# Score products and maxima of a windowed attention, contracted over 64 partitions in place of 128

## The reference

```python
scores = jnp.einsum('bhnqd,bhnkd->bhnqk', qw, kw) * scale + pos_bias[None, :, None]
probs = jax.nn.softmax(scores, axis=-1)
ow = jnp.einsum('bhnqk,bhnkd->bhnqd', probs, vw)
...
merged = merged / jnp.clip(counts, 1.0, None)[None, None, :, None]
ctx = merged.transpose(0, 2, 1, 3).reshape(Bb, Ss, Hid)
return ctx @ Wo + bo
```

## Time and profile before

| | |
|---|---|
| Time, median of 3 runs | 781.19 us (776.79 to 782.27) |
| The profiled execution | 777.4 us, its span 775.7 us |
| TensorE matmuls busy | 680.1 us, 88% |
| VectorE / ScalarE / GpSimd busy | 499.4 / 371.6 / 433.3 us |
| TensorE's mean granted clock | 0.948 of 2.4 GHz |

### The profile page before, as it was taken

How to read it: one execution, slowest core, us unless ns; L and a number is a source line. 1 busy time by engine, 2 the same in 40 slices (tenths; PEclk the granted TensorE clock), 3 DMA queues, 4 the chain that set the end, 5 groups by cost and what they waited for, 6 DMA issues and landing times. The chain is left out here.

```text
span 775.7 us, 34452 instructions
## 1 busy us (share of the span) xinstructions
PE 680.1 (88%) x13946; PEld 544.1 (70%) x13946; DVE 499.4 (64%) x1624; ACT 371.6 (48%) x546; POOL 433.3 (56%) x482
## 2 busy tenths in 40 slices
PE   4699999999999999999999999988999999999000
PEld 1467777767776777677777677768999999999000
DVE  6735656666675665756657557665788766766076
ACT  2133443443434434434343342445677777776058
POOL 6820334545545545455464454456777777777645
PEclk8889999999999999999999999998999999999555
DMA  6884436435454353443643534013434534332196
GB/s 156 241 266 122 126 92 170 130 88 151 123 146 138 94 169 112 120 143 112 164 135 86 159 110 131 26 38 88 147 101 117 157 101 112 103 106 69 48 381 269
DMA packets 84029, 103.61 MB, mean 134 GB/s; under 512 B 15937, under 2 KB 70593, under 8 KB 83873
## 3 DMA queue, kind: packets, MB, share of 16 engines
q1 hardware_dynamic: 73792, 82.26, 36.6%
q0 software_dynamic: 8640, 17.84, 7.2%
q10 hardware_dynamic: 1440, 1.31, 0.5%
HBM read 60.12 MB, written 40.79 MB: 130 GB/s over the span
## 5 line engine op out<-in xcount | busy, mean ns | idle before, releaser
L786 DVE TENSOR_REDUCE neg_max<-score_ps 128x16 f32<-128x1024 f32 x109 | 133.3, 1223 | 132.8 <-PE score_ps L1200 128.9
L295 POOL DMA_INDIRECT slots<-rows_sb,slot_at x128 | 128.0, 1000 | 154.6 <-PE o_ps L1253 119.2
L680 ACT ACTIVATE prob<-scoret_ps 128x1024 f32<-128x1024 f32 x112 | 114.6, 1023 | 143.6 <-PE scoret_ps L1200 143.6
L545 POOL DMA_INDIRECT results<-scaled_sb,result_at x142 | 136.2, 959 | 43.1 <-issue 35.2
L1253 PE MATMUL o_ps<-v_sb,prob 128*32 128x18 f32 x7168 | 90.6, 187 | 9.4 <-issue 8.6
L1253 PEld LDWEIGHTS o_ps<-v_sb,prob 128*32 128x32 f32 x7168 | 76.6, 110 | 22.0 <-issue 14.4
L713 ACT CAST w_slot<-wgu_sb 128x1024 fp32r x71 | 74.6, 1051 | 0.3 <-issue 0.3
L1237 PE MATMUL scoret_ps<-max_rows,half 128*64 128x512 bf16 x448 | 68.2, 382 | 5.3 <-DMA max_rows<-maxt_sb 5.1
L1220 PE MATMUL scoret_ps<-bias_hl,fold 128*64 128x512 f16 x448 | 70.2, 393 | 0.9 <-ACT prob L680 0.9
L1200 PE MATMUL scoret_ps<-blocks,stack 128*64 128x256 f16 x920 | 70.3, 274 | 0.1
L659 ACT COPY v_sb<-bank 64x512 f32<-64x512 f32 (+1 forms) x64 | 36.0, 563 | 68.4 <-PE bank L1190 38.6
(11 more groups left out here) (179 smaller groups left out, 1482.2 us busy)
## 6 DMA issues: line engine op xcount, KB each, us to landing
stack<-scratch SPq DMA_DIRECT2D x32, 512.0 KB
blocks<-scratch SPq DMA_DIRECT2D x126, 128.0 KB
scratch<-qk_hl SPq DMA_DIRECT2D x120, 128.0 KB
xin<-slots SPq DMA_DIRECT2D x71, 130.0 KB
blocks<-results SPq DMA_DIRECT2D x16, 512.0 KB, 6.3
x_sb<-in_x SPq DMA_DIRECT2D x16, 256.0 KB
out<-y_sb SPq DMA_DIRECT2D x16, 256.0 KB, 3.9
results<-scaled_sb,result_at POOLq DMA_INDIRECT x142, 2.6
```

Source lines behind the costliest of these rows:

```text
L295: nc.gpsimd.indirect_dma_start(slots, bass.IndirectOffsetOnAxis(ap=slot_at[:, k % 2, n:n + 1], axis=0), rows_sb[:, k % 2, n // TT, n % TT, ...
L545: pool.indirect_dma_start(results, bass.IndirectOffsetOnAxis(ap=result_at[s % RBUF][:, t:t + 1], axis=0), scaled_sb[:, s % RBUF, t, :], No ...
L680: act.activation(prob[:, (par + u) % 2, :], scoret_ps[:, :, :].rearrange("p b c -> p (b c)"), ACT.Exp).then_inc(exp_done, 1)
L786: dve.tensor_reduce(neg_max[:, par, v, :], ps[:, :, :].rearrange("p b (h k) -> p (b h) k", k=W), AX_X, ALU.max, negate=True).then_inc(max_ ...
```

## The change

The contraction is cut in two halves of 64 partitions. Each group of heads g gives two matmuls for each window where it gave one: n = 0 takes heads j = 0 and 1 on partitions 0 to 63 and writes bank 0, n = 1 takes j = 2 and 3 on partitions 64 to 127 and writes bank 1. Each has 128 columns. With the two windows (column halves of the array) that makes four tiles of 64 x 64. The maxima are laid out so that those of bank 0 come on partitions 0 and 1 and those of bank 1 on 64 and 65, and their matmul contracts over 64 partitions too. The order of heads, the mask, `neg_max` and the DMAs follow.

```diff
 def place(j, g):
-    return 4 * g + j
+    return 8 * (j // 2) + 2 * g + j % 2
...
-        neg_max = sb("neg_max", [P, 2, NU, H])
+        neg_max = sb("neg_max", [P, 2, 2, NU, H // 2])
...
-        max_rows = sb("max_rows", [P, NU * H, 64], BF16)
+        max_rows = sb("max_rows", [P, NU * H // 2, 64], BF16)
...
-                        sp.dma_start(max_rows[a:a + 1, :, :], maxt_sb[:, 64 * a:64 * a + 64]).then_inc(rows_in, 16)
+                        sp.dma_start(max_rows[a:a + 65:64, :, :], maxt_sb[:, 64 * a:64 * a + 64]).then_inc(rows_in, 16)
...
-                link(pool.memset(half[:, :], 1.0))
-                link(pool.affine_select(out=half[:, :], in_=half[:, :], compare_op=ALU.is_ge, fill=0.0, base=0,
-                                        pattern=[[1, P]], channel_multiplier=-64))
-                pool.affine_select(out=half[:, :], in_=half[:, :], compare_op=ALU.is_ge, fill=0.0, base=63,
-                                   pattern=[[-1, P]], channel_multiplier=64).then_inc(first_constants, 1)
+                windows = half[:, :].rearrange("p (a q) -> p a q", a=2)
+                link(pool.memset(half[:, :], 0.0))
+                link(pool.affine_select(out=windows, in_=windows, compare_op=ALU.not_equal, fill=1.0, base=0,
+                                        pattern=[[-1, 2], [0, 64]], channel_multiplier=1))
+                pool.affine_select(out=windows, in_=windows, compare_op=ALU.not_equal, fill=1.0, base=-64,
+                                   pattern=[[-1, 2], [0, 64]], channel_multiplier=1).then_inc(first_constants, 1)
...
-                    dve.tensor_reduce(neg_max[:, par, v, :], ps[:, :, :].rearrange("p b (h k) -> p (b h) k", k=W),
+                    dve.tensor_reduce(neg_max[:, par, :, v, :], ps[:, :, :].rearrange("p b (h k) -> p b h k", k=W),
...
                     for g in range(G):
-                        for a in range(2):
-                            t0 = UNITS[u][a]
-                            last = pe.matmul(ps[64 * a:64 * a + 64, g // 2, (g % 2) * 4 * W:(g % 2 + 1) * 4 * W],
-                                             stack[:, par, a_of, g, t0:t0 + W],
-                                             blocks[:, par, b_of, g, :, t0:t0 + W],
-                                             start=False, stop=True, skip_group_check=True)
+                        for n in range(2):
+                            k = slice(64 * n, 64 * n + 64)
+                            for a in range(2):
+                                t0 = UNITS[u][a]
+                                last = pe.matmul(ps[64 * a:64 * a + 64, n, 2 * g * W:2 * (g + 1) * W],
+                                                 stack[k, par, a_of, g, t0:t0 + W],
+                                                 blocks[k, par, b_of, g, 2 * n:2 * n + 2, t0:t0 + W],
+                                                 start=False, stop=True, skip_group_check=True)
...
-                            pe.matmul(scoret_ps[rows, n, :], half[:, rows],
-                                      max_rows[:, u * H + 8 * n:u * H + 8 * n + 8, :].rearrange("a h q -> a (h q)"),
+                            pe.matmul(scoret_ps[rows, n, :], half[64 * n:64 * n + 64, rows],
+                                      max_rows[64 * n:64 * n + 64, 8 * u:8 * u + 8, :].rearrange("p h q -> p (h q)"),
...
-                    pe.transpose(bank[0][0:NU * H, 0:P], neg_max[:, par, :, :].rearrange("p u h -> p (u h)"),
+                    pe.transpose(bank[0][0:NU * H, 0:P], neg_max[:, par, :, :, :].rearrange("p n u h -> p (n u h)"),
```

## The result

The changed kernel takes 790.33 us, the median of 5 runs (788.97 to 799.95), against 779.92 before (776.79 to 782.27). The ratio is 1.015, 95% interval 1.011 to 1.019: slower by one and a half per cent where 764 us and a gain were forecast, and just outside the range, which ended at 790.

A forecast was written before the change was run, and what follows sets the result against it. TensorE's instruction list was taken to bound each attention step. Turned side gains 33.3 us, straight side loses 14.4, code costs 2: 17 off 781 gives 764 us, range 724 to 790.

The forecast's parts named there:

- the one on code: Whole kernel: 3,584 more TensorE instructions make some 14 more code packets, costing 1.1 to 3.9 us, taken as 2.
- The check in the part on products: Product groups: values put out records 10 ns each, 16 products need 14.5 ns each, so instruction supply is no bound.
- The row halves run side by side: Maxima: four matmuls on two row and two column halves run in one round, 0.217 us against 0.433.
- The change of the row count: Between TensorE groups: switching between 128-row and 64-row tiles costs 0.10 us, bounded by 0 and 0.164.
- exposed loads: First weight load after a shape change: 0.02 us into long matmuls, 0.05 into short ones, 12.3 us in all.
- the turned side: Turned maxima and products: gains 2.92 us a step less 0.84 for shape changes, 33.3 us in 16 steps.
- the straight side: Straight products: gain 1.41 us a step, shape changes cost 0.72 and 1.65; 14.4 us lost in 15 steps.
- The cheap: Rival: a row-count change costs 0.05 us or nothing, giving 746 or 715 us; chance of 715 to 750: 0.18.
- the dear change: Rival: a row-count change costs up to 0.164 us, giving 788 us; chance of 775 to 790: 0.14.
- the halves in turn: Rival: row halves load weights in turn, 815 us, or matmuls take turns too, 839; chance of 800 to 839: 0.12.
- The covers: Reduction's split output, the maxima's DMA onto two partitions and its prologue clearing stay hidden and cost nothing.
- anything else: Remaining outcomes, such as TensorE's clock falling with sparser work; chance 0.04.

The follow-up runs named there:

- e5: The kernel before, unchanged, profiled again on another job's chip: 782.23 us (one run).
- e6: The changed kernel, unchanged, run again on another job's chip: 795.30 us, 1.013 of the kernel before.
- e11: The kernel before with the change on the turned side alone and the values in matmuls of 64 queries, not 32: 764.71 us, 0.978 of before.
- e4: The changed kernel with the values in matmuls of 64 queries in place of 32, half as many instructions there: 0.980 of the kernel before.
- e3: The kernel before with the change on the turned side alone (maxima and turned products over 64 rows), straight products as before: 1.011 of before.
- e1: The kernel before with products in 16 matmuls of 128 columns, still over all 128 rows (3,584 extra instructions, no new tile shape): 1.017 of before.
- e10: The changed kernel with straight bias ahead of turned maxima and values in matmuls of 64 queries: 752.13 us, 0.960 of the kernel before.

## Why the prediction was wrong

**The step that failed** is the one on code: "14 packets cost 1.1 to 3.9; I take 2." The change cost about 29 us of idle time (1.82 us a step in 16 steps, e5 and e6; 1.77 of it at the boundaries of packets), the lower clock behind some of the stops included; the first pair of profiles has 2.31 us a step. The count of 14 was right. The price was taken as a mean per packet from the kernel before, as if each packet brought its own small share of idle time. But it goes by a threshold: nearly nothing where 256 instructions last over about 3.9 us, and about the difference where they don't. So it isn't the 14 packets more that cost, but that every packet has less time: 45 of 84 stretches fall under the threshold where 17 of 73 did. The rows taken from before could have shown it. Its plain turn stood at 4.08, just above, but its stops at the boundary already came to 0.88 us a step, 14 us in 16 steps, four of them over 1 us, while the prediction counted 1.1 to 3.9 for packets of the same size; and 200 against 232 instructions in a shorter turn is a sum that could be done beforehand. The check in the part on products, 10 ns an instruction in the values, was of how fast TensorE takes instructions that are there, not of how fast they come.

**What held.** The row halves run side by side, which no row of before had shown. The change of the row count costs 0.10 as taken (a guess from the nearest row, so partly luck), with exposed loads of the sizes taken; 28.8 was left of a step where 28.7 was forecast (29.82 - 1.12). By the same prices the turned side without the straight one should leave a step 0.24 shorter (2.92 - 0.84 - 0.72 = 1.36 gained, against 1.12); measured it is 0.11 (e11 to e4) and nothing (e3 to e6). So the straight side earns about nothing on the array and costs half of the added code; that it isn't a loss comes from the products, which are cheaper than forecast (a group of four rounds takes 0.22, not 0.23, and its exposed load 0.02 to 0.03, not 0.05). The cheap and the dear change, and the halves in turn, were each refuted by the first timeline. None of the rivals was the one that came; the code stood in the sum as a term, with no rival of its own.

**The covers.** The reduction, the maxima's DMA and its clearing cost nothing, as said. TensorE's clock was named only under "anything else", for sparser work; it did fall in places, but behind stops of the code, and at most 0.44 of the 3.52 us lost a step in e6 have to do with it (1.13 of 3.69 in the long first run).

**Left open:** why one run of a kernel has more and longer stops than another (788.97 to 799.95; the longest one is that with the most time at the lower clock, of two profiled), and what lies in the 1.3 us ahead of a packet's transfer and the 1.5 behind it. Nor is it known what the stops away from the packets' boundaries wait for (0.2 to 1.5 us a step with values by 32), and why one chip has more of them. The threshold is read from stops and not set by an experiment of its own: no run varied the number of instructions while all else stayed, except e1.

## What to carry to other kernels

Count the instructions of a stretch against its time before you split matmuls: where TensorE had caught up with its code, 256 of them (each load of weights is one) took about 3.9 us in these runs, and a gain on paper below that turned into idle time marked "issue" in the middle of groups, a fixed number of instructions apart. Look at the densest stretches and not at the mean: over a whole step the changed kernel has 4.1 us for a packet (28.8 us and 7 packets), and still 45 of 84 stretches are too dense. Smaller tiles that run side by side give what they promise, 0.43 down to 0.24, less 0.12 to 0.15 for each change of the tile's shape, so put groups of one shape next to each other. Where the code is the bound, a form with fewer matmuls can win though it costs more array time (e4, e10).

## What the runs showed of the hardware

A change of the array's division by rows costs the same 0.10 us as one by columns, plus 0.02 to 0.05 for the load that can't be fetched ahead. Four tiles of 64 x 64 stream side by side (four matmuls of 512 columns in 0.24 us, exposed load included, against 0.43 in two tiles), and weights of 64 columns for 16-bit products load behind 128 streamed columns without showing (e1's 0.44). Code comes to TensorE in packets of 256 instructions; where it is late, in one in about 3.9 us (3.48 the shortest of 121), at a DMA share of 0.12 as at 0.44, and TensorE goes on 1.1 to 1.7 us behind the end of the packet's transfer.
